# Column sums of batch 1 taken on ScalarE from DMA-transposed blocks, with gate 1 and tile 2's y reordered around them

## The reference

```python
x = x + quantised_matmul(layernorm(x), ctx)          # both sides rounded to 0..255 around a zero point
x = x + ffn(layernorm(x))
# ffn: base = y @ W.T + b;  logits = y @ W_router.T;  top 2 of 8 experts, softmax weights
#      lora = ((y @ A.T) * weight of the expert) @ B * 2;  result = base + lora
```

## Time and profile before

| what | value |
|---|---|
| median of three runs | 168.48 us (168.28 to 168.65) |
| profiled execution, its own time | 168.88 us |
| span of that execution in the trace | 167.1 us |
| granted TensorE clock, mean | 0.997 |
| TensorE (PE) busy | 155.1 us, 93% of the span |
| VectorE (DVE) busy | 127.4 us, 76% |
| ScalarE (ACT) busy | 72.6 us, 43% |
| GpSimd (POOL) busy | 37.9 us, 23% |

### The profile page before, as it was taken

The page is one execution under the profiler, slowest core; times in us unless marked ns, Lnnn a source line. Parts: engine busy times, 40 slices in busy tenths (PEclk is TensorE's granted clock), DMA queues, the critical chain, the costliest instruction groups (busy, mean ns, idle before and its releaser), DMA issues.

```text
span 167.1 us, 2467 instructions
## 1 busy us (share of the span) xinstructions
PE 155.1 (93%) x875; PEld 80.5 (48%) x875; DVE 127.4 (76%) x283; ACT 72.6 (43%) x96; POOL 37.9 (23%) x113
## 2 busy tenths in 40 slices
PE   6858889879999999999999999999999999999990
PEld 3324335425446654644564456445644564555540
DVE  7988668999999989999889875988485828607702
ACT  3266699869999873225005300800080008003000
POOL 8204150343000433040614153125300040000000
PEclk9999999999999999999999999999999999999998
DMA  5999999991798523605430903291327002700311
GB/s 100 367 418 409 412 409 408 408 410 63 218 330 263 201 52 74 177 16 158 95 63 4 234 17 63 48 173 34 63 46 205 4 0 44 209 0 0 129 63 65
DMA packets 23677, 26.94 MB, mean 161 GB/s; under 512 B 17776, under 2 KB 18032, under 8 KB 23664
## 3 DMA queue, kind: packets, MB, share of 16 engines
q1 hardware_dynamic: 23520, 26.78, 50.8%
q10 hardware_dynamic: 144, 0.00, 0.0%
HBM read 18.38 MB, written 4.19 MB: 135 GB/s over the span
## 4 chain that ended last, share of the span: by engine, by line
PE 60%; DVE 12%; DMA 10%; ACT 9%; SPq 3%; issue 2%; POOL 2%; DVEq 0%; POOLq 0%
PE ps L889 37%; PE ps L840 10%; DMA xs<-in_x 7%; PE ps L877 6%; ACT w_hi L412 5%; DMA stage<-in_ctx_kv 3%; DVE w_lo L625 2%; SPq L208 2%; PE ps L868 2%; PE ps L870 2%; PE ps L869 2%; ACT a L366 1%; DVE a L556 1%; DVE ar_lo L619 1%; SPq L203 1%
## 5 line engine op out<-in xcount | busy, mean ns | idle before, releaser
L889 PE MATMUL ps<-w_hi,yt_hi 128*128 128x512 f16 x128 | 38.3, 380 | 0.9 <-ACT w_hi L412 0.9
L889 PE MATMUL ps<-w_hi,yt_lo 128*128 128x512 f16 x128 | 38.2, 379 | 0.0
L889 PE MATMUL ps<-w_lo,yt_hi 128*128 128x512 f16 x128 | 37.2, 379 | 0.0
L840 PE MATMUL ps<-a,a_t 128*128 128x512 f16 x128 | 30.1, 379 | 2.2 <-ACT a L366 0.9
L366 ACT ACTIVATE a<-stage,prm,inv_s 128x1024 uint8<-128x1024 f32 x16 | 19.5, 1241 | 9.5 <-DMA stage<-in_ctx_kv 9.2
L447 ACT ACTIVATE gate<-gate,ar_undo 128x1 f32<-128x1 f32 x8 | 2.4, 295 | 46.5 <-DVE gate L661 46.5
L840 PEld LDWEIGHTS ps<-a,a_t 128*128 128x128 f16 x128 | 12.2, 98 | 16.8 <-ACT a L366 1.4
L889 PEld LDWEIGHTS ps<-w_hi,yt_lo 128*128 128x128 f16 x128 | 12.5, 98 | 15.1 <-DVE yt_lo L638 0.2
L889 PEld LDWEIGHTS ps<-w_lo,yt_hi 128*128 128x128 f16 x128 | 12.5, 98 | 14.1
L889 PEld LDWEIGHTS ps<-w_hi,yt_hi 128*128 128x128 f16 x128 | 11.5, 98 | 15.0 <-issue 2.1
L293 POOL TENSOR_SCALAR root<-mvy 128x1 f32<-128x1 f32 x8 | 1.9, 234 | 57.7 <-DVE mvy L514 57.7
(11 more groups left out here) (138 smaller groups left out, 248.1 us busy)
## 6 DMA issues: line engine op xcount, KB each, us to landing
stage<-in_ctx_kv SPq DMA_DIRECT2D x16, 512.0 KB, 5.5
stage<-in_w_t SPq DMA_DIRECT2D x8, 512.0 KB, 13.0
xs<-in_x SPq DMA_DIRECT2D x7, 512.0 KB, 12.0
out_dram<-xs SPq DMA_DIRECT2D x7, 512.0 KB, 3.0
ar_raw<-in_ar_t SPq DMA_DIRECT2D x1, 544.0 KB, 13.7
xs<-in_x SPq DMA_DIRECT2D x2, 256.0 KB, 3.8
b_raw<-in_b_t SPq DMA_DIRECT2D x1, 512.0 KB, 12.5
bias_sb<-in_bias SPq DMA_DIRECT2D x1, 512.0 KB, 13.3
```

Of the source, the lines that this page charges most:

```text
L840: last = nc.tensor.matmul(ps[:, s1_bank(t) + h, :], a1_t[:, t % 4, k, :], a2[:, k, h * H:(h + 1) * H], start=k == 0, stop=k == K - 1)
L889: ins = nc.tensor.matmul(ps[:, OUT_BANK[p] + h, :], part, rhs[:, k, h * H:(h + 1) * H], start=k == 0 and i == 0, stop=stop and i == 2)
```

## The change

Batch 1's column sums leave TensorE. SP transposes each of the 8 quantised context blocks of batch 1 by DMA into the first half of its staging slot (which the quantised block has freed), so that a column of the context lies along the free axis of a partition. ScalarE then sums one group of 128 columns at a time, over all 8 blocks, with an accumulator (`sum_columns`, 8 instructions of 128x1024). TensorE spreads the sums over all partitions with 8 f32 matmuls against the identity, the sums as broadcast weights (`spread_columns`, 4 after k = 1 and 4 after k = 4 of tile 2's wide product), into bank 3, and ScalarE makes the correction in two halves (`make_later_corr`). The first correction stays as it was (`make_first_corr`). Stage 1 of the late tiles no longer waits for the correction.

Four of the new transposes stand in SP's queue ahead of tile 2's high half, one between its halves, three behind. On ScalarE the y pass of tile 2, gate 1 and the first split move ahead of the last context block; the sums stand among the work for tiles 2 and 3. On VectorE gate 1 moves ahead of tile 2's low half, and the statistics and quantisation of x 4 move behind the second split and behind the output sum of tile 0.

```diff
--- before.py
+++ after.py
@@ -74,6 +74,7 @@
         b_lo = sb("b_lo", [P, D], F32R)
         y = sb("y", [P, D], F32)
         y_hi = sb("y_hi", [P, D], F16)
+        col_sum = sb("col_sum", [P, K], F32)
         y_lo = sb("y_lo", [P, D], F16)
         yt_hi = sb("yt_hi", [P, 2, K, P], F16)
         yt_lo = sb("yt_lo", [P, 2, K, P], F16)
@@ -131,6 +132,9 @@
         def a1_bank(t):
             return 4 + t % 2
 
+        def turned_ctx(k):
+            return stage[:, k, 0:H].bitcast(F16).rearrange("p (j r) -> p j r", j=K)
+
         def low_bytes(tile):
             return tile.bitcast(U8)[:, 0:2 * D:2]
 
@@ -138,6 +142,7 @@
             return 3 if t == 1 else 2
 
         COLSUM_BANK = 6
+        SPREAD_BANK = 3
         WARM_BANK = 5
         PEAK_BANK = 4
         YT_BANKS = slice(6, 8)
@@ -177,7 +182,8 @@
         yt_hi_ready, yt_lo_ready = sem("yt_hi_ready"), sem("yt_lo_ready")
         y_hi_ready, y_lo_ready = sem("y_hi_ready"), sem("y_lo_ready")
         yt_hi_in, yt_lo_in = [sem(f"yt_hi_in{i}") for i in range(2)], [sem(f"yt_lo_in{i}") for i in range(2)]
-        a1t_in = sem("a1t_in")
+        a1t_in, ctx_turned = sem("a1t_in"), sem("ctx_turned")
+        columns_summed, columns_spread = sem("columns_summed"), sem("columns_spread")
         ar_done = sem("ar_done")
         gate_diff, gate_exp, hc_ready = sem("gate_diff"), sem("gate_exp"), sem("hc_ready")
         hc_transposed, hct_hi_ready, hct_lo_ready = sem("hc_transposed"), sem("hct_hi_ready"), sem("hct_lo_ready")
@@ -257,10 +263,19 @@
                 sp.wait_ge(out_summed, t + 1)
                 sp.dma_start(out_tiles[t], xs[:, t, :]).then_inc(stored, 16)
 
+            def turn_ctx(n):
+                sp.wait_ge(ctx_ready, n + 1)
+                sp.dma_start_transpose(turned_ctx(n - K), a2[:, n - K, :]).then_inc(ctx_turned, 16)
+
             for n in range(K, N):
                 load_ctx(n)
+            for n in range(K, K + 4):
+                turn_ctx(n)
             transpose_y_hi(2)
+            turn_ctx(K + 4)
             transpose_y_lo(2)
+            for n in range(K + 5, N):
+                turn_ctx(n)
             transpose_a1(4)
             store(0)
             for t in range(2, T - 1):
@@ -366,11 +381,25 @@
                 nc.scalar.activation(low_bytes(a2[:, n % K, :]), stage[:, n % RING, :], ACT.Identity,
                                      bias=prm[:, 3:4], scale=inv_s[:, 2:3]).then_inc(ctx_ready, 1)
 
-            def make_corr(b):
-                act.wait_ge(colsum_done, b + 1)
-                nc.scalar.activation(corr[:, b, :].rearrange("p (h n) -> p h n", h=NH),
+            def make_later_corr(h):
+                act.wait_ge(columns_spread, h + 1)
+                nc.scalar.activation(corr[:, 1, h * H:(h + 1) * H], ps[:, SPREAD_BANK, :], ACT.Identity,
+                                     bias=col_bias, scale=col_scale).then_inc(corr_ready, 1)
+
+            def make_first_corr():
+                act.wait_ge(colsum_done, 1)
+                nc.scalar.activation(corr[:, 0, :].rearrange("p (h n) -> p h n", h=NH),
                                      ps[:, COLSUM_BANK:COLSUM_BANK + NH, :], ACT.Identity,
                                      bias=col_bias, scale=col_scale).then_inc(corr_ready, 1)
+
+            def sum_columns(j):
+                act.wait_ge(ctx_turned, 16 * K)
+                act.wait_ge(rows_summed, 2)
+                if j > 1:
+                    act.wait_ge(columns_summed, j - 1)
+                turned = stage[:, :, 0:H].bitcast(F16).rearrange("p k (j r) -> p k j r", j=K)
+                nc.scalar.activation(junk[:, j % 2, :].rearrange("p (k r) -> p k r", k=K), turned[:, :, j, :],
+                                     ACT.Copy, accum_out=col_sum[:, j:j + 1]).then_inc(columns_summed, 1)
 
             def sum_row(t):
                 act.wait_ge(x_quantised, t + 1)
@@ -378,6 +407,7 @@
                 act.wait_ge(ar_peaks, 2)
                 if t >= 2:
                     act.wait_ge(rows_summed, t - 1)
+                    act.wait_ge(columns_summed, K)
                 nc.scalar.activation(junk[:, t % 2, :], a1[:, t, :], ACT.Copy, bias=-OFFSET - MIDDLE,
                                      accum_out=rowsum[:, t:t + 1]).then_inc(rows_summed, 1)
 
@@ -459,7 +489,7 @@
                 quantise_ctx(n)
             peaks_ar()
             act.wait_ge(consts_ready, 2)
-            make_corr(0)
+            make_first_corr()
             peak_of_first_w()
             for k in range(2, K):
                 peak_of_w(k)
@@ -474,16 +504,27 @@
             sum_row(0)
             quantise_ctx(K + 5)
             gate_weight(0)
-            for n in range(K + 6, N):
-                quantise_ctx(n)
+            quantise_ctx(K + 6)
             make_y_hi(2)
+            gate_weight(1)
             split_hct(0)
             make_y(2)
-            gate_weight(1)
+            quantise_ctx(K + 7)
+            split_hct(1)
             sum_row(1)
-            split_hct(1)
-            make_corr(1)
-            for t in range(2, T):
+            for j in range(5):
+                sum_columns(j)
+            gate_weight(2)
+            sum_columns(5)
+            make_y_hi(3)
+            make_y(3)
+            make_later_corr(0)
+            sum_columns(6)
+            sum_columns(7)
+            split_hct(2)
+            make_later_corr(1)
+            sum_row(2)
+            for t in range(3, T):
                 gate_weight(t)
                 if t + 1 < T:
                     make_y_hi(t + 1)
@@ -502,7 +543,7 @@
 
             def add_corr(t):
                 dve.wait_ge(x1_summed, t + 1)
-                dve.wait_ge(corr_ready, t // TB + 1)
+                dve.wait_ge(corr_ready, 1 if t < TB else 3)
                 nc.vector.tensor_tensor(xs[:, t, :], xs[:, t, :], corr[:, t // TB, :], ALU.add).then_inc(x1_ready, 1)
                 dve.wait_ge(x1_ready, t + 1)
 
@@ -768,14 +809,14 @@
             statistics_y(2)
             gate_tile(0)
             split_b()
-            statistics_x(4)
+            gate_tile(1)
             split_hct(0)
             make_y_lo(2)
-            gate_tile(1)
+            split_hct(1)
+            statistics_x(4)
+            add_bias(0)
+            sum_out(0)
             quantise_x(4)
-            add_bias(0)
-            split_hct(1)
-            sum_out(0)
             add_corr(3)
             statistics_y(3)
             centre_a1t(4)
@@ -833,6 +874,17 @@
                 if k == K - 1:
                     last.then_inc(colsum_done, 1)
 
+            def spread_columns(h):
+                pe.wait_ge(columns_summed, 4 * h + 4)
+                if h == 1:
+                    pe.wait_ge(corr_ready, 2)
+                for i in range(4):
+                    j = 4 * h + i
+                    last = nc.tensor.matmul(ps[:, SPREAD_BANK, i * P:(i + 1) * P],
+                                            col_sum[:, j:j + 1].to_broadcast([P, P]), ident[:, :],
+                                            start=True, stop=True)
+                last.then_inc(columns_spread, 1)
+
             def product(t, k):
                 n = t // TB * K + k
                 pe.wait_ge(ctx_ready, n + 1)
@@ -844,7 +896,6 @@
 
             def late_product(t):
                 pe.wait_ge(a1t_ready, t + 1)
-                pe.wait_ge(corr_ready, 2)
                 pe.wait_ge(x1_summed, t)
                 for k in range(K):
                     product(t, k)
@@ -950,10 +1001,7 @@
                     transpose_hc(0)
             pe.wait_ge(b_lo_ready, 1)
             lora(0, stop=True)
-            for k in range(K):
-                column_sums(1, k)
-                if k == 3:
-                    transpose_hc(1)
+            transpose_hc(1)
             lora(1, stop=True)
 
             for t in range(2, T - 1):
@@ -963,6 +1011,10 @@
                 pe.wait_ge(out_summed, t - 1)
                 for k in range(K):
                     wide(t, k, k == K - 1)
+                    if t == 2 and k == 1:
+                        spread_columns(0)
+                    if t == 2 and k == 4:
+                        spread_columns(1)
                     if k == 2 and t + 2 < T:
                         late_product(t + 2)
                     if k == 3:
```

## The result

The changed kernel takes 174.91 us (median of 4 runs, 174.55 to 175.46) against 168.56: a ratio of 1.0377, 95% interval [1.0338, 1.0416], so 6.35 us slower where 3.5 was forecast, and 0.5 us above the range. The sign and the place were right, the size was not. The profiled execution took 174.55 us, with a span of 172.7.

What follows compares the result with a forecast made beforehand. TensorE, busy without slack from 70.8 to 163 us, was taken as the bound; 3.4 us of work away, 2.2 of spreads and more idling gave +3.5 on the median 168.48: 172.0 us, range 169.8 to 174.4.

Steps and rivals of the forecast that it cites:

- TensorE's early gain: Before tile 2's wide product: sixteen matmuls, about 3.4 us, go, and LoRA 1 starts at about 64.85, 3.0 us earlier.
- what is late next: Tile 2's wide product waits for VectorE's output sum of tile 0, starting at 69.0, not 70.8: 1.8 us left.
- The turned sums: Last transpose lands at 70.2, the fourth sum is readable at 74.7; TensorE idles 3.1 us at the first spread.
- I take that they cost it nothing: In SP's queue, the first five new transposes are done before y low comes at 63.4, without delaying it.
- The last lands 3.0 after 67.15: The eighth transpose in SP's queue, issued at 67.15, lands at 70.2.
- slow transposes as a rival of 0.08: Transposes in a row take 2.20 to issue, 4.7 to land; the last lands 3.6 us later: 175.6 us, chance 0.08.
- a rival at 0.12: TensorE's clock falls in the stall to half pace, losing 1.9 us: about 173.9 us, chance 0.12.
- The spreads: Eight f32 matmuls on TensorE at 0.28 us each, 2.2 us in all, bounds 1.1 and 3.4.
- The sum: Adding up TensorE's terms: k 2 of tile 2 starts 2.4 us later, the other four spreads add 1.1: +3.5 us.
- What I called hidden: The wait for tile 4, centred at 74.4 after x 4's move, falls inside the spread stall and costs nothing more.

Runs made afterwards that it cites:

- Experiment 2: The changed kernel with 22 unused 128x512 matmuls on TensorE between k 1 and the first spreads: 172.88 us, ratio 1.0251 to the kernel before.
- Experiments 4 and 5: 4: the changed kernel's orders with batch 1's column sums back on TensorE, 170.45 us; 5: the same with x 4's statistics ahead of split 1, 168.72 us.
- experiment 1: The changed kernel with the two groups of spreads moved from behind k 1 and k 4 to behind k 3 and k 6: 178.55 us, ratio 1.0513.
- experiment 7: The kernel before without batch 1's 16 column-sum matmuls and with nothing in their place: 170.62 us, ratio 1.011.
- experiment 9: The kernel before without batch 1's column sums and with split 1 ahead of tile 0's bias on VectorE: 168.62 us, ratio 1.0011.
- experiment 6: The kernel before with the eight context transposes added to SP's queue in the changed kernel's places, read by nobody: 168.97 us, ratio 1.0023.
- experiment 10: The changed kernel with spreads behind k 3 and k 7, gate 2 behind three sums, row sum 2 before the second correction half: 172.6 us.

## Why the prediction was wrong

*TensorE's early gain, and what is late next: right.* With the 0.46 by which this execution was ahead, LoRA 1 was due at 64.4 and the wide product at 68.5; they came at 64.25 and 68.53.

*The turned sums: the step that failed.* The last transpose was to land at 70.2, which is 69.7 in this execution's time, 1.0 either way. ScalarE's first sum, which waits for it, starts at 71.99: 2.2 later. Two sentences had it wrong. "I take that they cost it nothing" was said of the first five transposes; but four of them stood behind context loads, took 8.20 us to issue, and pushed y high, a fifth, y low and the last three back. Those three then came 1.38 apart, not 1.25, so the eighth was issued at 67.72 where 66.7 was due: 1.0. And "The last lands 3.0 after 67.15" took the landing of a single transpose: with others in flight ahead of it the eighth took 4.2: 1.2. The four sums were 0.2 quicker than taken, and TensorE came to the spreads 0.2 later, so the gap was 5.0 instead of 3.1: +1.9. I had slow transposes as a rival of 0.08, 3.6 us late, and put its price into no bound; a little over half of that came true, the landing (4.2 against its 4.7) and not the issue of the last three (1.38 against its 2.20).

*The clock: a rival at 0.12 that happened.* It cost 0.97 in the spreads and 0.56 in k 2: +1.5, close to the 1.9 priced. Experiment 2 took the idling away, and the clock stayed. Its condition was the size of the gap, which the first error made longer; whether the clock would have fallen in the 3.1 us that I forecast, no run shows. The Trainium skill ("TensorE: Matmul & The Clock Gate", section "HAM oscillation — how this bites in real kernels") says that long idle gaps throttle the array. The trace agrees for the gap of 5.0 us.

*The spreads: a size.* 0.22 each (0.89 for four), against 0.28 taken: -0.5. The Trainium skill ("FP8 and Floating Point Precision", section "TensorE Precision Notes") gives a true f32 product four passes. The estimate worked out from that was 0.235; the trace agrees.

*The sum.* Tile 3's router product was due at 86.13 - 0.46 + 3.5 = 89.2 in this execution's time and came at 92.36, 3.2 later. The terms give 1.9 for the gap, 0.2 for TensorE's later arrival, 1.5 for the clock and -0.5 for the spreads: 3.1. The mechanism stood; two terms were short. This accounts for the stretch in the traces, where the two executions are 5.67 apart at their ends; that the medians, 6.35 apart, come as near to 3.5 + 1.9 + 1.5 - 0.5 = 6.4 is in part luck.

*What I called hidden.* The effect of x 4's move was hidden only by the gap. Experiments 4 and 5 show it at 1.7 us once the gap is gone: VectorE, with 0.6 us of slack at LoRA 2, is the next bound, and I had read TensorE's full windows as if nothing else were near. So it was with gate 2, which I had ScalarE's sums delay by about 1 us: it waited 2.67, and experiment 1 shows such a wait as 3.00 at LoRA 2.

*What none of these versions collects.* The 3.4 us of matmuls were no loss to win back here. They ran while LoRA 1 waited for gated rows 1, and kept the clock up (experiment 7); with that wait shortened, doing without them still gave nothing, at either clock (experiment 9). Spreads of 1.8 us that stand in the way replaced them. Why the eighth transpose landed in 4.2 us rather than 3.0 was not taken apart further; that transposes in a row hold each other up is what the rows of the changed kernel and of experiment 6 show, not a mechanism.

## What to carry to other kernels

Work on the bounding engine that lies in one of its waits cost nothing here, and even paid: ask what the engine would do in that time instead before taking it away. A transfer placed in a queue can delay all that is issued behind it, and an engine that waits for it in program order passes the delay on to unrelated work, here gate 2 on ScalarE. A stretch read as "no slack on engine A" says nothing of engine B's 0.6 us.

## What the runs showed of the hardware that was not expected

The granted clock fell to 0.50 after a gap of 5.0 us, and also after waits of 1.78 and 2.10 us with a single 0.33 us turn between them (experiment 7), and after 1.78 and 0.69 (experiment 9, in the traced execution; three of its twelve executions have a mean clock of 1.00). It stayed at 1.00 through a single wait of 1.65 between full stretches (experiment 10). A DMA transpose issued at 53.97, while context loads were still in flight (ScalarE waited for one of them until 56.81), held its queue for 3.95 us, where one issued alone took 1.23; why was not taken apart.
